# A kernel of one state-space layer and a mixture of experts: the order in which its tiles are allocated in SBUF

## The reference, cut to what matters

```
# stage 1, per sequence x (512 x 128)
z = x @ Wz;  B, C, dt_raw, X = split(x @ Win)          # X: 8 heads of 64
delta = softplus(dt_raw + dt_bias)
h_t = exp(-delta_t * exp(A_log)) * h_(t-1) + X_t (x) (delta_t * B_t);  y_t = h_t . C_t
v = ((y + D * X) * (silu(z) @ Wzg)) @ Wout;  x1 = layernorm(x + v)
# stage 2, per token
dw = combined top-3 softmax weights of 3 routers over 12 experts
o = sum_e dw[e] * (W2[e] @ gelu(sum_e dw[e] * (W1[e] @ x1)) + b2[e]);  out = layernorm(x1 + o)
```

## Time and profile before

| | us |
|---|---|
| median of 3 runs | 1543.08 |
| lowest and highest | 1542.68, 1543.85 |
| the profiled execution's own time | 1543.08 |
| its span, first to last instruction | 1541.4 |
| PE busy | 1525.5 |
| DVE busy | 1114.1 |
| POOL busy | 657.1 |
| ACT busy | 597.9 |

### The profile page before, as it was taken

One profiled execution on the slowest core, in us unless ns is written; L12 is line 12 of the kernel. 1 busy time (PEld: TensorE's weight loads), 2 busy tenths in 40 slices (PEclk: granted clock), 3 DMA queues, 4 the chain that ended last, 5 costly groups with the idle time before them and its releaser, 6 DMA issues.

```text
span 1541.4 us, 25335 instructions
## 1 busy us (share of the span) xinstructions
PE 1525.5 (99%) x8646; PEld 1249.8 (81%) x8646; DVE 1114.1 (72%) x3113; ACT 597.9 (39%) x1360; POOL 657.1 (43%) x751
## 2 busy tenths in 40 slices
PE   9999999999999999999999999999999999999998
PEld 7778888888888888888788888888888888887886
DVE  7677776877768787686776768777686776868755
ACT  6643424425244351533525244242443515335130
POOL 6671623616145270643616336162451705436040
PEclk9999999999999999999999999999999999999999
DMA  5341312304023140321404123140231403214020
GB/s 180 100 148 29 117 43 67 100 29 134 19 76 91 30 137 15 103 71 46 120 12 124 46 63 104 28 132 22 73 94 28 138 15 97 76 40 128 13 78 7
DMA packets 81456, 114.53 MB, mean 74 GB/s; under 512 B 10144, under 2 KB 37296, under 8 KB 81328
## 3 DMA queue, kind: packets, MB, share of 16 engines
q1 hardware_dynamic: 81328, 112.92, 24.7%
HBM read 107.76 MB, written 5.13 MB: 73 GB/s over the span
## 4 chain that ended last, share of the span: by engine, by line
PE 92%; POOL 3%; DVE 1%; issue 1%; DMA 1%; SPq 1%; ACT 0%; POOLq 0%; DVEq 0%; ACTq 0%
PE exp_bank L246 22%; PE exp_bank L248 22%; PE exp_bank L247 22%; PE mix_bank L895 4%; PE mix_bank L921 3%; PE mix_bank L246 3%; PE mix_bank L248 3%; PE mix_bank L247 3%; PE mix_bank L903 3%; PE mix_bank L792 1%; PE turn_bank L1248 1%; POOL w_lo L444 1%; PE mix_bank L738 1%; PE mix_bank L1012 1%; PE mix_bank L524 1%
## 5 line engine op out<-in xcount | busy, mean ns | idle before, releaser
L1189 POOL TENSOR_TENSOR sp_lo<-fbuf,sp_hi 128x512 fp32r<-128x512 f32 (+2 forms) x201 | 243.0, 1213 | 178.4 <-ACT sp_hi L1185 108.5
L246 PE MATMUL exp_bank<-w_hi,sp_hi 128*128 128x512 f32 x768 | 304.0, 396 | 0.8 <-POOL sp_lo L1241 0.8
L246 PE MATMUL exp_bank<-sp_hi,w_hi 128*128 128x512 f32 x764 | 303.3, 397 | 0.2
L248 PE MATMUL exp_bank<-w_hi,sp_lo 128*128 128x512 f32 x768 | 299.7, 390 | 0.0
L247 PE MATMUL exp_bank<-w_lo,sp_hi 128*128 128x512 f32 x768 | 298.9, 389 | 0.0
L248 PE MATMUL exp_bank<-sp_hi,w_lo 128*128 128x512 f32 x764 | 298.2, 390 | 0.0
L247 PE MATMUL exp_bank<-sp_lo,w_hi 128*128 128x512 f32 x764 | 297.6, 389 | 0.0
L1288 DVE SCALAR_TENSOR_TENSOR acc<-exp_bank,dw,acc 128x128 f32<-128x128 f32 x384 | 132.2, 344 | 137.4 <-PE exp_bank L248 136.7
L1185 ACT CAST sp_hi<-fbuf 128x512 fp32r<-128x512 f32 (+2 forms) x203 | 119.9, 592 | 273.5 <-DVE fbuf L1155 218.1
L855 POOL TENSOR_TENSOR Wt<-Wt,Gh 128x512 f32<-128x512 f32 x128 | 184.8, 1445 | 21.1 <-DVE Wt L847 21.1
L246 PEld LDWEIGHTS exp_bank<-sp_hi,w_hi 128*128 128x128 f32 x764 | 143.6, 188 | 38.5 <-issue 8.9
(11 more groups left out here) (267 smaller groups left out, 2284.7 us busy)
## 6 DMA issues: line engine op xcount, KB each, us to landing
row_b<-dw_rows SPq DMA_DIRECT2D x189, 256.0 KB, 3.4
seg_b<-dA_rows SPq DMA_DIRECT2D x124, 256.0 KB, 3.5
ctd<-cum_rows SPq DMA_DIRECT2D x128, 96.0 KB, 3.1
x_in<-in_x SPq DMA_DIRECT2D x16, 256.0 KB, 2.7
result<-acc SPq DMA_DIRECT2D x15, 256.0 KB, 2.2
fbuf<-in_W1T SPq DMA_DIRECT2D x12, 256.0 KB, 3.7
acc<-in_W2T SPq DMA_DIRECT2D x5, 256.0 KB, 3.4
x_in<-in_W2T SPq DMA_DIRECT2D x5, 256.0 KB, 2.9
```

Source lines behind the costliest of these rows:

```text
L246: nc.tensor.matmul(ps, s_hi, m_hi, start=start and j == 0, stop=False, skip_group_check=onto)
L248: last = nc.tensor.matmul(ps, s_lo, m_hi, start=False, stop=stop and j == n - 1, skip_group_check=onto)
L1189: sig("xw_lo", on.tensor_tensor(lo[:, cols], wide[e % 2][:, cols], hi[:, cols].bitcast(F32), ALU.subtract))
```

## The change

The change alters the order of the calls of `sb` and leaves out `before_lines`. No instruction is added, removed or moved: the rows on PE (5680), DVE (2131), ACT (805), POOL (630) and SP (377) stand in the same order, with the same tiles, shapes and semaphores. What differs is the SBUF address that every instruction and every transfer carries. Tiles in PSUM keep theirs.

```diff
-        sb("before_lines", [P, 32])
+        w1_hi, w1_lo = sb("w1_hi", [P, E, HID], F32R), sb("w1_lo", [P, E, HID], F32R)
+        w2_hi, w2_lo = sb("w2_hi", [P, NH, E * D], F32R), sb("w2_lo", [P, NH, E * D], F32R)
+
+        wbc_hi, wbc_lo = sb("wbc_hi", [P, 2 * NS], F32R), sb("wbc_lo", [P, 2 * NS], F32R)
+        wz_hi, wz_lo = sb("wz_hi", [P, DZ], F32R), sb("wz_lo", [P, DZ], F32R)
+        wx_hi, wx_lo = sb("wx_hi", [P, DI], F32R), sb("wx_lo", [P, DI], F32R)
+        wzg_hi, wzg_lo = sb("wzg_hi", [P, NK, DI], F32R), sb("wzg_lo", [P, NK, DI], F32R)
+
+        wbdt = sb("wbdt", [P, NS + H])
         wout = sb("wout", [P, NQ, D])
+        router = sb("router", [P, NR * E])
         b2_sb = sb("b2_sb", [P, NC, D])
...
         strict_r = sb("strict_r", [P, P], F32R)
+        iota_i, iota_e = sb("iota_i", [P, E], I32), sb("iota_e", [P, E])
+        bias_b, neg_a, d_b = sb("bias_b", [P, H]), sb("neg_a", [P, H]), sb("d_b", [P, H])
...
         dt_s = sb("dt_s", [P, 6, NC * H])
+        delta, a_rows = sb("delta", [P, NC, H]), sb("a_rows", [P, H, NC])
+        a = a_rows[:, :, :].rearrange("p h c -> p c h")
+        a_hi, a_lo = sb("a_hi", [P, NC, H], F32R), sb("a_lo", [P, NC, H], F32R)
+        ends = sb("ends", [P, (NC - 1) * H])
+        total = sb("total", [P, NC * NQ])
```

More of the change, by code:

```diff
@@ L136, in layer_program @@
         sp_hi, sp_lo = sb("sp_hi", [P, NH, T], F32R), sb("sp_lo", [P, NH, T], F32R)
[L137 to L143, removed]
         lg = fbuf[:, 3, 0:NC * NR * E].rearrange("p (g e) -> p g e", e=E)
@@ L151, in layer_program @@
         st6, mv, nrm = sb("st6", [P, NC, 6]), sb("mv", [P, NC, 2]), sb("nrm", [P, 6, NC])
[L152 to L160, removed]
         xb = [ctx.enter_context(nc.psum_tensor(f"mix_bank{n}", [P, T], F32)) for n in range(NX)]
```

## The result

The changed kernel takes 1562.65 us (median of 4 runs, 1561.91 to 1562.97). The kernel before takes 1542.88 us in the 4 runs beside it. The ratio is 1.0127, with a 95% interval of 1.0112 to 1.0141. That is 19.8 us slower, where the prediction said 1543.3 us.

What follows compares the result with a forecast made beforehand. PE was taken to bound the kernel, busy throughout steady batches. 1543.08 us + 0.2 in the start + 0 in steady batches + 0 at PE = 1543.3 us; range for 8 in 10: 1541.5 to 1550.5 us.

Steps and rivals of the forecast that it cites:

- Bound and counts: Steady batches: PE is busy throughout; no instruction comes, goes or moves, so no term for counts, queues or new waits.
- Transfers: Landings at shifted destinations: 0.1 us more per 256 KB transfer, hidden in steady batches, 2 x 0.1 = 0.2 us in the start.
- the gap in the start: PE's idle 2.43 us at 94.22 us, waiting for `Wt` from POOL; forecast at 2.4 to 2.8 us after the change.
- mostly latency: Argument against the rival of slower transfers (1.0 us more a landing, 1546.1 us, chance 0.13): a landing's time is mostly latency.
- The rule of the Trainium skill: Transactions start at 256-byte boundaries; 9% more on the 2.0 us byte part makes `row_b` 0.19 us longer, sum 1543.5 us.
- DVE, ACT and POOL: Their reads and writes at shifted addresses: 0 taken, covered by PE; 3.1 us at the most for DVE without that cover.
- PE's reads ... I take 0: PE reading operands at shifted addresses: 0 taken, ends 0 and 1 ns an instruction, 8646 x 1 ns = 8.6 us.
- The moving operands stay at multiples of 64: Argument against PE reading more slowly: the moving operands of the expert products stay at multiples of 64 bytes.
- PE reads more slowly: Rival in every product: 1 ns on each of 8646 instructions gives 1551.7 us; chance 0.09.
- what would show it: Signs in the changed profile; for slower PE reads, 512-column products of 390 ns or more (389 before) with no new waits.

Runs made afterwards that it cites:

- The last two grids: Kernels of PE alone, without the reference's work: offsets down to 4 bytes, other widths and types (297.05 us); then narrower weights, fewer rows and columns, single odd products (240.88 us).

## Why the prediction was wrong

**Bound and counts: right.** PE bounds every batch, nothing moves, and no wait is new.

**Transfers: right.** They were given 0.1 us each, hidden except in the start. `row_b` takes no longer, `seg_b` 0.1 us more, which it also does where it wasn't moved, and the gap in the start has not grown. The kernel with only the weights at 128 takes them out for good: it is as slow with no destination moved. (One argument doesn't follow from the prediction's own rows: transfers are not "mostly latency" where 1.4 of 3.4 us don't go with the bytes. Nothing hung on it.) The rule of the Trainium skill that the prediction weighed (DMA: Bandwidth & Descriptors, "How a descriptor splits into AXI transactions") would give 0.19 us more for `row_b`. The trace has 3.4 us before and after, so it is smaller here than one digit of the row. That page speaks of bytes that are fetched, while here it is the destination that begins off a boundary.

**DVE, ACT and POOL: right.** Their busy times rose by 0.5, 0.8 and 1.7 us, under PE's cover.

**"PE's reads ... I take 0": this step failed.** It is a term of the sum that was mis-sized, and it is the whole error: 19.1 us on 5328 products, 3.6 ns on the mean one, where 0 was taken and 8.6 us was the upper end. Two things in its working were wrong. First, the value came from products of 36 and 72 columns in plain float32, which aren't fp32r products of 512. The prediction says itself that they tell little of a long read, and it still put its bound at the 1 ns between them. The last two grids show that float32 products of 512 columns don't depend on the offset, and that fp32r ones of 256 are no slower off it (118 against 120 ns). So rows of short float32 products could hardly have shown the effect. A bound from rows of another shape and type isn't a bound. Second, each operand's start was looked at alone, where the distance of the two decides. "The moving operands stay at multiples of 64" stood against the rival, though 64 is one of the dear distances.

**The rival that was right and too small.** *PE reads more slowly*, with a chance of 0.09 and 1551.7 us, is what happened: products longer, no new wait, a longer batch, each as "what would show it" had it. It missed by 11 us, because 1 ns an instruction on all 8646 stood for what is 1.5 ns in one kind (3.3 us of 2246), 5.5 in the other (12.3 us of 2244) and next to nothing in the 3318 that aren't fp32r products of 512 columns.

The Trainium skill would not lead one to expect this: its page SBUF — State Buffer, "Who interferes with whom", calls the two read ports of PE, for the moving operand and for the weights, independent, and PE an engine that never waits on anyone. In this kernel the products lose 6 ns when only the distance of these two reads changes, at the same 188 ns of load. The measurement decides, though no run shows that the ports are the place. By that page, the PE term would have been 0, as the prediction took it.

## What to carry to other kernels

Where PE is the bound with fp32r products of 128x512, put the moving and the stationary tile at SBUF addresses that differ by a multiple of 256 bytes; one filler of 192 bytes was worth 15 us of 1563 here. The weights of the next product count as much as a product's own, so give all tiles that PE reads in turns the same remainder. Compare two kernels' addresses before comparing their times, as a reordered list of tiles can move a time by 1.3% with the same instructions. In the profile, this shows as longer mean products with no new wait, and start-to-start distances in the timeline give its price.

## What was unexpected of the hardware

- fp32r products of 128x512 start every 226.7 ns if the two addresses differ by a multiple of 256 bytes, every 229 ns at a difference of 192, and every 232 to 234 ns at the other multiples of 32. 4 bytes off are enough.
- bfloat16 (215.8 ns) and float32 (858 ns) products of 512 columns don't depend on it.
- Products that fit in themselves, but whose moving operand doesn't fit the weights of the next, are slower still: 236.5 ns.
- With fewer columns it is otherwise: 448 columns take 206.0 ns at a difference of 0 and 199.9 at 192, 256 columns 120 and 118, and 192 or 128 columns 110 to 112 ns at all four differences tried.
- One product at another pair of addresses, though fitting in itself, slows the 8 behind it from 227 to 231 ns.
